# Flamingo block on one core: small loads on Sync's queue, an early activation table, score scale and gate folded into earlier operands, flag work ahead of unit 2's maxima

## The chip, the cores and the metric

The kernel runs on one core of a Trainium2 chip. The metric is device time in microseconds (us), start to end of one execution; a median of several runs is given. Lower is better. The profile is one more execution of the same program, recorded by the hardware profiler.

## The reference, cut to what matters

The input `x` is 2 x 1024 tokens of width 256. Four residual steps follow each other; the change touches the first and the two gates of the others:

```python
x = x + jnp.tanh(g_xattn[0]) * xattn0(_layernorm(x), ctx, ctx, W, b)   # one head, q = k = v projection
x = x + jnp.tanh(g_ffn[0])   * ffn0(_layernorm(x), Wg, Wu, Wd)          # 8 experts of 1024, all of them summed
x = x + jnp.tanh(g_xattn[1]) * xattn1(_layernorm(x), ctx, mask, ...)    # 8 heads, masked keys
x = x + jnp.tanh(g_ffn[1])   * moe1(_layernorm(x), wg, W, b)            # top-1 routing
# xattn0:
q, k, v = query @ W.T + b, key @ W.T + b, value @ W.T + b
weights = softmax(q @ k.T / sqrt(256)); out = weights @ v
```

The context has 154 rows for each of the two batches. `tanh(g_ffn)` is multiplied by a flag for each batch that says whether its mask leaves any key.

## The kernel before, in words

The 2048 tokens are 16 tiles of 128 rows; four tiles make a unit, so there are four units (u = 0 to 3). The kernel has five instruction streams written out by hand, one for each engine, tied by semaphores; each stream runs strictly in its written order. There are three stages: the first attention (0 to about 54 us), the dense experts of the first feed-forward (54 to about 999 us, 64 groups of matmuls in split precision), and the second attention with the routed experts (to the end).

First attention. Keys and values are the same projection k0 of the context, so the scores are computed as normalised x times A0 = W^T k0, plus a row r0 = b k0. The order of work at the start:

- Sync's queue issues the load of W0 (L495), of x unit by unit (L497) and of the first two quarters of expert weights (L506 to L508).
- ScalarE's stream issues eight loads (L893 to L900: context, bias, two gate rows, gamma, beta, gate weights, mask), then copies the transposed weight (W0T, L904) and half of the transposed context (ctxT, L906) out of PSUM, adds the bias into half of k0T (L909), takes tanh of the gates (L911, after all six loads counted by `small_in`), normalises unit 0 (L916, with rstd and shift that GpSimd makes, L601 and L603), copies half of A0 (L966), xnT (L923), V0 (L970), and for each unit the exponentials (L929) and the transposed probabilities (L936).
- TensorE runs some matmuls without use to keep busy (L1270), transposes W0 (L1278) and the context (L1283), makes k0T (L1290), r0 (L1323) and A0 (L1327), transposes unit 0 (L1296) and the values (L1314), then for each unit scores (L1340 adds r0, L1345), transposes of the probabilities (L1353) and the attention itself (L1360). The scores of unit u wait for the additions of unit u-2 (`a_res`).
- VectorE copies the other half of ctxT (L1921), takes the variances of each unit (L1879, L1883, L1886), makes the other half of k0T (L1925), splits r0 into three bfloat16 rows (L1929 to L1936), copies half of A0 (L1938), takes the maxima of the scores (L1947) and scales them (L1952), forms the coefficient tanh(g)/den (L1959, L1961) and adds the attention to x (L1968). The flag work (L1989 to L1995, here behind `a_maxes(2)` and `ln2_variances(0)`) reduces the mask and multiplies the gates. L1978, L464 and L490 prepare the first operands of the experts.
- GpSimd copies the bias rows (L590), takes powers for the normalisations (L595, L601), converts the mask (`mask_rows`, L753), and splits the first experts' weights into high and low parts (L619 to L632, and w_lo in L642, L644, L648).

Of the kernel before, what the change touches and what calls it, by code (L numbers as in the profile page):

```python
# [16 lines left out]
F32 = mybir.dt.float32  # L17
# [72 lines left out]
def flamingo_kernel(nc, x, ctx, mask, g_xattn, g_ffn, W0, b0, Wg, Wu, Wd, gamma, beta, Wq, Wkv, Wout, wgate, We, be, out):  # L90
# [55 lines left out]
    NORMED0, A0_OUT, V0_OUT, NORMED20 = 5, 6, 8, 9  # L146
# [31 lines left out]
    with ExitStack() as stack:  # L178
# [63 lines left out]
        nmA, nmsA, denA, rdenA, coefA = (sa.take(n, [P, NT], F32) for n in ("nmA", "nmsA", "denA", "rdenA", "coefA"))  # L242
# [3 lines left out]
        sr = Arena(nc, sa.at - 4 * CT * D, sa.at)  # L246
        bcol_rows = sr.take("bcol_rows", [P, KB, R_ROWS], F32)
# [246 lines left out]
        def _(sp):  # L494
# [3 lines left out]

            def load_weights(q):
# [60 lines left out]
        def _(pool):  # L560
# [29 lines left out]
            nc.gpsimd.tensor_copy(bcol_rows[:, :, 0:R_ROWS:R_MID], bcol[:].unsqueeze(2).to_broadcast([P, KB, 3])).then_inc(bias_ready, 1)  # L590
# [301 lines left out]
        def _(act):  # L892
            act.dma_start(ctx_s[:], ctx_v).then_inc(ctx_in, 16)  # L893
            act.dma_start(bcol[:], b0.rearrange("(k p) -> p k", p=P), allow_slow_non_contiguous=True).then_inc(b0_in, 16)
            act.dma_start(graw[:, 0:2], g_xattn.rearrange("(a g) -> a g", a=1).partition_broadcast(P)).then_inc(small_in, 16)
            act.dma_start(graw[:, 2:4], g_ffn.rearrange("(a g) -> a g", a=1).partition_broadcast(P)).then_inc(small_in, 16)
            act.dma_start(gammac[:], gamma.rearrange("(k p) -> p k", p=P), allow_slow_non_contiguous=True).then_inc(small_in, 16)
            act.dma_start(betac[:], beta.rearrange("(k p) -> p k", p=P), allow_slow_non_contiguous=True).then_inc(small_in, 16)
            act.dma_start(wgr[:], wgate.rearrange("(k p) e -> p k e", p=P)).then_inc(small_in, 16)
            act.dma_start(mask8[:], mask.rearrange("(a b) k -> a (b k)", a=1).partition_broadcast(P)).then_inc(small_in, 16)  # L900
# [9 lines left out]
            act.wait_ge(small_in, 96)  # L910
            nc.scalar.activation(tg[:], graw[:], ACT.Tanh).then_inc(prep_act, 1)  # L911

# [12 lines left out]
            def a_exps(u):  # L925
                act.wait_ge(a_nmax, u + 1)
                for j in range(CT):
                    n = u * CT + j
                    ins = nc.scalar.activation(PA[:, u % 2 * CT + j, :], bank[UNIT_PS[u % 2][j // 2]][:, j % 2 * 256:j % 2 * 256 + KEYS], ACT.Exp,  # L929
                                               bias=nmsA[:, n:n + 1], scale=D ** -0.5, accum_out=denA[:, n:n + 1])  # L930
# [35 lines left out]
            nc.scalar.copy(A0[:, 0, :], bank[1][:, 0:AK]).then_inc(prep_act, 1)  # L966
            a_xnT_out(0)
            for i in range(2):
# [1556 lines left out]
```

## Time and profile before

| | us |
|---|---|
| median of 3 runs | 1227.21 |
| lowest and highest | 1225.78, 1228.43 |
| profiled execution, span from the first to the last instruction | 1225.2 |
| TensorE busy in it | 1199.5 |
| VectorE busy | 1051.4 |
| GpSimd busy | 886.6 |
| ScalarE busy | 739.6 |

The span leaves out what lies ahead of the first and behind the last instruction. Busy time is summed over the span; which engine limits a stage is read from the stage, by who waits for whom. PE is TensorE's matmul, PEld its weight load, DVE VectorE, ACT ScalarE, POOL GpSimd, SP Sync; a q behind a name is that engine's sequencer or its queue of DMA issues.

### The profile page before, as it was taken

What the parts mean: (1) busy time and instruction counts of PE and PEld (TensorE: products, weight loads), DVE (VectorE), ACT (ScalarE), POOL (GpSimd) and SP (SyncE); (2) the same over time, 40 slices, a digit from 0 to 9 for tenths busy, and PEclk for the clock granted to TensorE, in tenths of its full rate; (3) what the DMA queues carried; (4) which work ended last, traced back from release to release, by engine and by line L of the source; (5) the groups of instructions that cost most, each with busy time, mean ns of one, the idle gap of its engine ahead of it and who ended that gap; (6) DMA issues with size and microseconds to landing.
All of it is one profiled execution on the core that took longest, in us unless ns stands there. A gap on an engine that the chain in (4) does not pass through costs nothing.

```text
span 1225.2 us, 18428 instructions
## 1 busy us (share of the span) xinstructions
PE 1199.5 (98%) x6143; PEld 987.8 (81%) x6143; DVE 1051.4 (86%) x1754; ACT 739.6 (60%) x1531; POOL 886.6 (72%) x848
## 2 busy tenths in 40 slices
PE   8999999999999999999999999999999998999998
PEld 6778888888888888888888888888888887777776
DVE  6887899999999999999999999999999874767556
ACT  4775566666666666666666666666666545545544
POOL 4575688888888888878888888888888626444435
PEclk9999999999999999999999999999999999999999
DMA  4020301000000000000000000011000330000131
GB/s 142 26 95 25 98 13 39 27 26 26 27 26 27 26 27 26 27 26 27 27 26 27 26 27 26 27 38 40 27 26 1 120 121 1 19 26 11 36 96 70
DMA packets 42365, 48.27 MB, mean 39 GB/s; under 512 B 4239, under 2 KB 40143, under 8 KB 42015
## 3 DMA queue, kind: packets, MB, share of 16 engines
q1 hardware_dynamic: 38992, 43.33, 10.7%
q0 software_dynamic: 1440, 3.41, 0.7%
q8 instruction: 49, 0.80, 0.3%
q10 hardware_dynamic: 1839, 0.37, 0.2%
q14 instruction: 45, 0.37, 0.1%
HBM read 37.36 MB, written 10.29 MB: 39 GB/s over the span
## 4 chain that ended last, share of the span: by engine, by line
PE 89%; DVE 5%; ACT 3%; issue 1%; ACTq 1%; POOL 0%; POOLq 0%; DVEq 0%
PE bank L1400 25%; PE bank L1402 25%; PE bank L1401 25%; ACT PC L1124 3%; PE bank L1643 2%; PE bank L1652 1%; PE bank L1822 1%; DVE nmC L2204 1%; PE bank L1805 1%; PE bank L1345 1%; PE bank L1755 1%; DVE stats L1879 1%; PE bank L1577 1%; PE bank L1627 1%; PE bank L1578 1%
## 5 line engine op out<-in xcount | busy, mean ns | idle before, releaser
L1400 PE MATMUL bank<-xop_hi,w_hi 128*128 128x512 f32 x896 | 349.2, 390 | 1.9 <-DVE half_g L2028 0.9
L1402 PE MATMUL bank<-xop_hi,w_lo 128*128 128x512 f32 x896 | 348.6, 389 | 0.0
L1401 PE MATMUL bank<-xop_lo,w_hi 128*128 128x512 f32 x896 | 348.6, 389 | 0.0
L2063 DVE TENSOR_TENSOR hid_lo<-hid,hid_hi 128x512 fp32r<-128x512 f32 x228 | 232.5, 1044 | 6.0 <-ACT hid_hi L1042 6.0
L1400 PEld LDWEIGHTS bank<-xop_hi,w_hi 128*128 128x128 f32 x896 | 168.2, 188 | 37.9 <-DVE half_g L2028 1.3
L1402 PEld LDWEIGHTS bank<-xop_hi,w_lo 128*128 128x128 f32 x896 | 168.2, 188 | 35.0
L1401 PEld LDWEIGHTS bank<-xop_lo,w_hi 128*128 128x128 f32 x896 | 168.2, 188 | 34.7
L1042 ACT CAST hid_hi<-hid 128x512 fp32r<-128x512 f32 x228 | 140.8, 622 | 63.6 <-PE bank L1402 38.3
L1026 ACT ACTIVATE s<-bank 128x512 f32<-128x512 f32 x128 | 78.2, 611 | 95.2 <-PE bank L1402 95.2
L1400 PE MATMUL bank<-hid_hi,wd_hi 128*128 128x512 f32 x344 | 134.2, 390 | 0.7 <-DVE hid_lo L2063 0.6
L1401 PE MATMUL bank<-hid_lo,wd_hi 128*128 128x512 f32 x344 | 133.9, 389 | 0.0
L1402 PE MATMUL bank<-hid_hi,wd_lo 128*128 128x512 f32 x344 | 133.9, 389 | 0.0
L1002 ACT COPY bank<-bank 128x512 f32<-128x512 f32 x128 | 73.2, 573 | 67.9 <-PE bank L1402 67.9
L2087 DVE TENSOR_TENSOR acc<-bank,acc 128x512 f32<-128x512 f32 x136 | 93.0, 684 | 20.4 <-PE bank L1402 20.3
L1032 ACT ACTIVATE half_g<-half_g 128x512 f32<-128x512 f32 x128 | 81.1, 634 | 46.8 <-DVE half_g L2036 25.5
L2055 DVE TENSOR_TENSOR hid<-half_u,half_g 128x512 f32<-128x512 f32 x128 | 107.2, 875 | 0.0
L702 POOL TENSOR_TENSOR t_loT<-t_rawT,t_hiT 128x512 fp32r<-128x512 f32 x56 | 84.2, 1526 | 16.4 <-ACT t_hiT L1049 16.4
L2046 DVE TENSOR_TENSOR hid<-bank,s 128x512 f32<-128x512 f32 x128 | 86.6, 676 | 1.2 <-PE bank L1402 1.2
L648 POOL TENSOR_TENSOR w_lo<-w_raw,w_hi 128x1024 fp32r<-128x1024 f32 x32 | 77.5, 2421 | 2.9 <-ACT w_hi L1063 2.9
L796 POOL TENSOR_TENSOR PC<-PC,rdenC 128x616 f32<-128x616 f32 x32 | 38.9, 1216 | 53.5 <-DVE rdenC L2212 53.4
L1400 PEld LDWEIGHTS bank<-hid_hi,wd_hi 128*128 128x128 f32 x344 | 64.6, 188 | 15.3 <-DVE hid_lo L2063 1.0
L1402 PEld LDWEIGHTS bank<-hid_hi,wd_lo 128*128 128x128 f32 x344 | 64.6, 188 | 13.5
(288 smaller groups left out, 2608.3 us busy)
## 6 DMA issues: line engine op xcount, KB each, us to landing
raw_gu<-in_L_ffn_Wg_dram SPq DMA_DIRECT2D x32, 256.0 KB, 2.7
raw_gu<-in_L_ffn_Wu_dram SPq DMA_DIRECT2D x32, 256.0 KB, 3.1
raw_d<-in_L_ffn_Wd_dram SPq DMA_DIRECT2D x32, 256.0 KB, 3.6
slots<-empty_row SPq DMA_DIRECT2D x1, 2080.0 KB, 11.2
xr<-slots SPq DMA_DIRECT2D x8, 260.0 KB, 4.5
x_res<-in_x_dram SPq DMA_DIRECT2D x4, 512.0 KB, 8.9
x_mid<-x_res SPq DMA_DIRECT2D x1, 2048.0 KB, 7.4
x_res<-x_mid SPq DMA_DIRECT2D x4, 512.0 KB, 5.4
```

Of the source, the lines that this page charges most:

```text
L648: nc.gpsimd.tensor_tensor(out=lo[:, :, W_S1:W_S4 + 1], in0=s[:, :, W_S1:W_S4 + 1], in1=hi[:, :, W_S1:W_S4 + 1].bitcast(F32), op=ALU.subtra ...
L702: nc.gpsimd.tensor_tensor(out=t_lo[i][:], in0=t_raw[i][:], in1=t_hi[i][:].bitcast(F32), op=ALU.subtract).then_inc(t_ready, 1)
L1026: nc.scalar.activation(out[:], ps[:], ACT.Silu).then_inc(silu_ready[h], 1)
L1032: nc.scalar.activation(half["g"][:], half["g"][:], ACT.Silu).then_inc(silu_ready[h], 1)
L1042: nc.scalar.copy(hid_hi[n % 2][h][:], hid[h][:]).then_inc(hi_ready[h], 1)
L1400: mm(ps, w, a, start=start, stop=False, skip_group_check=True)
L1401: mm(ps, w, a_low, start=False, stop=False, skip_group_check=True)
L1402: return mm(ps, w_low, a, start=False, stop=True, skip_group_check=True)
L2046: nc.vector.tensor_tensor(out=hid[h][:], in0=ps[:], in1=s[:], op=ALU.mult).then_inc(hid_ready[h], 1)
L2055: nc.vector.tensor_tensor(out=hid[h][:], in0=half["u"][:], in1=half["g"][:], op=ALU.mult).then_inc(hid_ready[h], 1)
L2063: nc.vector.tensor_tensor(out=hid_lo[n % 2][h][:], in0=hid[h][:], in1=hid_hi[n % 2][h][:].bitcast(F32), op=ALU.subtract).then_inc(lo_ready ...
L2087: nc.vector.tensor_tensor(out=to, in0=ps, in1=to, op=ALU.add).then_inc(acc_added, 1)
```

## The change

Six loads (two gate rows, mask, gamma, beta, gate weights) are issued by Sync behind the four x loads, ahead of the expert weights, instead of by ScalarE. ScalarE's stream begins, after its two remaining loads, with an exponential of one column. The tanh of the gates moves behind the copies of unit 0's transposes and ahead of the value copies. The factor 256^-0.5 goes into A0 and into the bias rows behind r0, so that the scores come out scaled, and the scaling of the maxima (L1952) goes. The first gate goes into the values V0, so that the coefficient (L1961) goes. The flag work stands ahead of unit 2's maxima. The semaphore counts of `prep_act` are renumbered. The diff, cut to its core:

```diff
@@ -143,7 +143,7 @@
     V_BANKS = ((6, 7, 0), (1, 2, 7))
     C_VALUES = 2 + HB // 2
     PREP_DVE = 4
-    NORMED0, A0_OUT, V0_OUT, NORMED20 = 5, 6, 8, 9
+    NORMED0, A0_OUT, GATES, V0_OUT, NORMED20 = 4, 5, 6, 8, 9
     R_MID, R_LOW = 32, 64
     R_ROWS = R_LOW + 1
     PREP_PE = 10
@@ -239,11 +239,12 @@
         xnT = sa.take("xnT", [P, 2, KB, CH], F32)
         PA = sa.take("PA", [P, 2 * CT, KEYS], F32)
         PTA = sa.take("PTA", [KH, 2, 2, CH], F32)
-        nmA, nmsA, denA, rdenA, coefA = (sa.take(n, [P, NT], F32) for n in ("nmA", "nmsA", "denA", "rdenA", "coefA"))
+        nmA, denA, rdenA = (sa.take(n, [P, NT], F32) for n in ("nmA", "denA", "rdenA"))
         mask8 = sa.take("mask8", [P, AK], U8, size=1)
         maskf = sa.take("maskf", [P, AK], F32)
         xnA = sa.take("xnA", [P, NT, D], F32)
         sr = Arena(nc, sa.at - 4 * CT * D, sa.at)
+        early_table = sa.take("early_table", [P, 1], F32)
         bcol_rows = sr.take("bcol_rows", [P, KB, R_ROWS], F32)
         r0_rest = sr.take("r0_rest", [R_ROWS, AK], F32)
         sums_at = sa.at + (OPERANDS_AT - sa.at) % ROW_BYTES
@@ -496,6 +497,13 @@
             for u in range(NC):
                 sp.dma_start(x_res[:, u * CT:(u + 1) * CT, :], x_v[:, u * CT:(u + 1) * CT, :]).then_inc(x_in[u], 16)
 
+            sp.dma_start(graw[:, 0:2], g_xattn.rearrange("(a g) -> a g", a=1).partition_broadcast(P)).then_inc(small_in, 16)
+            sp.dma_start(graw[:, 2:4], g_ffn.rearrange("(a g) -> a g", a=1).partition_broadcast(P)).then_inc(small_in, 16)
+            sp.dma_start(mask8[:], mask.rearrange("(a b) k -> a (b k)", a=1).partition_broadcast(P)).then_inc(small_in, 16)
+            sp.dma_start(gammac[:], gamma.rearrange("(k p) -> p k", p=P), allow_slow_non_contiguous=True).then_inc(small_in, 16)
+            sp.dma_start(betac[:], beta.rearrange("(k p) -> p k", p=P), allow_slow_non_contiguous=True).then_inc(small_in, 16)
+            sp.dma_start(wgr[:], wgate.rearrange("(k p) e -> p k e", p=P)).then_inc(small_in, 16)
+
             def load_weights(q):
                 e, f = q // (NQ // NE0), q % (NQ // NE0)
                 if q >= 2:
@@ -587,7 +595,8 @@
             nc.gpsimd.affine_select(out=before[:], in_=before[:], compare_op=ALU.is_gt, fill=0.0, base=0,
                                     pattern=[[1, P]], channel_multiplier=-1).then_inc(consts_ready, 1)
             pool.wait_ge(b0_in, 16)
-            nc.gpsimd.tensor_copy(bcol_rows[:, :, 0:R_ROWS:R_MID], bcol[:].unsqueeze(2).to_broadcast([P, KB, 3])).then_inc(bias_ready, 1)
+            nc.gpsimd.tensor_scalar(bcol_rows[:, :, 0:R_ROWS:R_MID], bcol[:].unsqueeze(2).to_broadcast([P, KB, 3]),
+                                    D ** -0.5, None, ALU.mult).then_inc(bias_ready, 1)
 
             def power(lane, n, count, first=0):
                 pool.wait_ge(var_ready[lane], count)
@@ -892,12 +901,8 @@
         def _(act):
             act.dma_start(ctx_s[:], ctx_v).then_inc(ctx_in, 16)
             act.dma_start(bcol[:], b0.rearrange("(k p) -> p k", p=P), allow_slow_non_contiguous=True).then_inc(b0_in, 16)
-            act.dma_start(graw[:, 0:2], g_xattn.rearrange("(a g) -> a g", a=1).partition_broadcast(P)).then_inc(small_in, 16)
-            act.dma_start(graw[:, 2:4], g_ffn.rearrange("(a g) -> a g", a=1).partition_broadcast(P)).then_inc(small_in, 16)
-            act.dma_start(gammac[:], gamma.rearrange("(k p) -> p k", p=P), allow_slow_non_contiguous=True).then_inc(small_in, 16)
-            act.dma_start(betac[:], beta.rearrange("(k p) -> p k", p=P), allow_slow_non_contiguous=True).then_inc(small_in, 16)
-            act.dma_start(wgr[:], wgate.rearrange("(k p) e -> p k e", p=P)).then_inc(small_in, 16)
-            act.dma_start(mask8[:], mask.rearrange("(a b) k -> a (b k)", a=1).partition_broadcast(P)).then_inc(small_in, 16)
+            act.wait_ge(pool_steps, 1)
+            nc.scalar.activation(early_table[:], ones_r[:, 0:1], ACT.Exp)
 
 
             act.wait_ge(prep_pe, 1)
@@ -907,9 +912,6 @@
             act.wait_ge(prep_pe, 5)
             act.wait_ge(b0_in, 16)
             nc.scalar.activation(k0T[:, 1, :], bank[4][:, 0:AK], ACT.Identity, bias=bcol[:, 1:2], scale=1.0).then_inc(prep_act, 1)
-            act.wait_ge(small_in, 96)
-            nc.scalar.activation(tg[:], graw[:], ACT.Tanh).then_inc(prep_act, 1)
-
             def a_norm(u, count):
                 act.wait_ge(rstd_ready[u], count)
                 for j in range(CT):
@@ -927,7 +929,7 @@
                 for j in range(CT):
                     n = u * CT + j
                     ins = nc.scalar.activation(PA[:, u % 2 * CT + j, :], bank[UNIT_PS[u % 2][j // 2]][:, j % 2 * 256:j % 2 * 256 + KEYS], ACT.Exp,
-                                               bias=nmsA[:, n:n + 1], scale=D ** -0.5, accum_out=denA[:, n:n + 1])
+                                               bias=nmA[:, n:n + 1], accum_out=denA[:, n:n + 1])
                 ins.then_inc(a_probs, 1)
 
             def a_pT_out(u):
@@ -963,11 +965,15 @@
 
             a_norm(0, 1).then_inc(prep_act, 1)
             act.wait_ge(prep_pe, 7)
-            nc.scalar.copy(A0[:, 0, :], bank[1][:, 0:AK]).then_inc(prep_act, 1)
+            nc.scalar.mul(A0[:, 0, :], bank[1][:, 0:AK], D ** -0.5).then_inc(prep_act, 1)
             a_xnT_out(0)
+            act.wait_ge(small_in, 96)
+            nc.scalar.activation(tg[:], graw[:], ACT.Tanh).then_inc(prep_act, 1)
+            act.wait_ge(prep_act, GATES)
             for i in range(2):
                 act.wait_ge(prep_pe, 9 + i)
-                nc.scalar.copy(V0[:, 2 * i:2 * i + 2, :].rearrange("p k d -> p (k d)"), bank[V0_PS[i]][0:KH, :]).then_inc(prep_act, 1)
+                nc.scalar.mul(V0[:, 2 * i:2 * i + 2, :].rearrange("p k d -> p (k d)"), bank[V0_PS[i]][0:KH, :],
+                              tg[0:KH, 0:1]).then_inc(prep_act, 1)
             a_xnT_out(1)
             a_exps(0)
             a_pT_out(0)
@@ -1935,7 +1941,7 @@
             own()
             nc.vector.tensor_tensor(out=r0[low, :], in0=r0_rest[low, :], in1=r0[low, :], op=ALU.subtract).then_inc(prep_dve, 1)
             dve.wait_ge(prep_pe, 8)
-            nc.vector.tensor_copy(A0[:, 1, :], bank[2][:, 0:AK]).then_inc(prep_dve, 1)
+            nc.vector.tensor_scalar(A0[:, 1, :], bank[2][:, 0:AK], D ** -0.5, None, ALU.mult).then_inc(prep_dve, 1)
             ln1_normed(1)
             ln1_variances(2)
 
@@ -1946,19 +1952,12 @@
                     n = u * CT + 2 * i
                     ins = nc.vector.reduce_max(nmA[:, n:n + 2], bank[UNIT_PS[u % 2][i]][:].rearrange("p (a k) -> p a k", a=2)[:, :, 0:KEYS],
                                                AX.X, negate=True)
-                steps.did(ins)
-                own()
-                us = slice(u * CT, (u + 1) * CT)
-                nc.vector.tensor_scalar(nmsA[:, us], nmA[:, us], D ** -0.5, None, ALU.mult).then_inc(a_nmax, 1)
-
-            def a_coefs(u):
+                ins.then_inc(a_nmax, 1)
+
+            def a_rdens(u):
                 us = slice(u * CT, (u + 1) * CT)
                 dve.wait_ge(a_probs, u + 1)
-                if u == 0:
-                    dve.wait_ge(prep_act, 4)
                 steps.did(nc.vector.reciprocal(rdenA[:, us], denA[:, us]))
-                own()
-                steps.did(nc.vector.tensor_scalar(coefA[:, us], rdenA[:, us], tg[:, 0:1], None, ALU.mult))
 
             def a_add_half(u, half):
                 own()
@@ -1966,11 +1965,11 @@
                 for j in range(2 * half, 2 * half + 2):
                     x = unit(u)[j]
                     ins = nc.vector.scalar_tensor_tensor(out=x, in0=bank[UNIT_PS[u % 2][half]][:, j % 2 * D:(j % 2 + 1) * D],
-                                                         scalar=coefA[:, u * CT + j:u * CT + j + 1], in1=x, op0=ALU.mult, op1=ALU.add)
+                                                         scalar=rdenA[:, u * CT + j:u * CT + j + 1], in1=x, op0=ALU.mult, op1=ALU.add)
                 ins.then_inc(a_res, 1)
 
             def a_add(u):
-                a_coefs(u)
+                a_rdens(u)
                 for half in range(2):
                     a_add_half(u, half)
 
@@ -1983,9 +1982,8 @@
             a_maxes(1)
             ln1_variances(3)
             a_add(0)
-            a_maxes(2)
-            ln2_variances(0)
             dve.wait_ge(bias_ready, MASK_READY + 1)
+            dve.wait_ge(prep_act, GATES)
             steps.did(nc.vector.reduce_max(anyv[:], maskf[:].rearrange("p (b k) -> p b k", b=B), AX.X))
             own()
             steps.did(nc.vector.reciprocal(ranyv[:], anyv[:]))
@@ -1994,6 +1992,8 @@
             own()
             steps.did(nc.vector.tensor_scalar(tg_ffn[:], tg[:, 2:4], flag[:, 0:1], flag[:, 1:2], ALU.mult, ALU.mult))
             own()
+            a_maxes(2)
+            ln2_variances(0)
             a_add(1)
             ln2_variances(1)
             a_maxes(3)
```

## Rows read from the trace of the kernel before

**Rows 1.** The page, its chain that ended last: share of the span by engine.

```profile
PE 89%; DVE 5%; ACT 3%; issue 1%; ACTq 1%; POOL 0%; POOLq 0%; DVEq 0%
```

**Rows 2.** Busy time by stretch: length, then PE, PEld, DVE, ACT, POOL, clock, DMA.

```profile
0.00:54.00 54.00, 48.19 (x274) 38.53 (x274) 38.25 (x115) 29.99 (x78) 27.10 (x67) 0.97 0.30 95
...
66.00:999.00 933.00, 932.02 (x4116) 770.84 (x4116) 855.60 (x1133) 584.20 (x1043) 746.04 (x679) 1.00 0.11 36
```

**Rows 3.** Timeline, 5 to 18 us: start, length, engine, line; in brackets idle time.

```profile
5.33 1.01 PE L1278 MATMUL bank<-ident,W0s 128*128 128x128 f32 x4
...
7.88 1.28 ACT L904 ACT_TABLE_LOAD   x1 [7.88 <-issue]
...
9.66 0.42 ACT L906 COPY ctxT<-bank 128x308 f32<-128x308 f32 x1
...
10.13 3.72 PE L1290 MATMUL bank<-ctxT,W0T 128*128 128x308 f32 x8 [2.83 <-ACT ctxT L906]
...
11.03 0.20 POOL L603 TENSOR_TENSOR shift<-shift,rstd 128x4 f32<-128x4 f32 x1
...
13.89 0.52 ACT L909 ACTIVATE k0T<-bank,bcol 128x308 f32<-128x308 f32 x1 [3.81 <-PE bank L1290]
...
14.40 2.06 ACT L916 ACTIVATE xnA<-x_res,shift,rstd 128x256 f32<-128x256 f32 x4
...
14.51 1.22 PE L1323 MATMUL bank<-k0T,bcol_rows 128*65 128x308 f32 x4
...
15.57 2.24 PE L1327 MATMUL bank<-k0T,W0s 128*128 128x308 f32 x8
```

**Rows 4.** Busy time by stretch, as rows 2, while L1290 runs.

```profile
9.60:12.90 3.30, 2.77 (x6) 1.89 (x7) 0.23 (x1) 0.48 (x2) 1.48 (x3) 0.50 1.11 342
```

**Rows 5.** Timeline, 31 to 41 us.

```profile
31.43 0.88 DVE L1968 SCALAR_TENSOR_TENSOR x_res<-bank,coefA,x_res 128x256 f32<-128x256 f32 x2 [0.18 <-PE bank L1360]
...
34.47 1.60 DVE L1952 TENSOR_SCALAR nmsA<-nmA 128x4 f32<-128x4 f32 x1
...
37.90 0.47 DVE L1989 TENSOR_REDUCE anyv<-maskf 128x2 f32<-128x308 f32 x1
...
40.62 0.29 PE L1340 MATMUL bank<-r,ones_r 65*128 65x308 bf16 x1 [1.39 <-DVE x_res L1968]
```

**Rows 6.** Timeline of VectorE, 6 to 16 us, and the second x load, with its landing.

```profile
6.91 0.48 DVE L1921 COPY ctxT<-bank 128x308 f32<-128x308 f32 x1 [6.91 <-PE bank L1283]
...
13.13 1.39 DVE L1879 BATCH_NORM_STATS2 stats<-x_res 128x6 f32<-128x256 f32 x4
...
15.77 0.47 DVE L1929 CAST r<-bank 65x308 bf16<-65x308 f32 x1 [0.63 <-PE bank L1323]
...
L497 SPq DMA_DIRECT2D x_res<-in_x_dram x1: 502/502/502, 1.8 to 1.8; - x1
...
DMA to landing us min/median/max: 8.4/8.4/8.4
```

**Rows 7.** Timeline of issues, 1 to 6 us, wgr's landing, and ScalarE at 21.74.

```profile
1.91 0.48 ACTq L895 DMA_DIRECT2D graw<-in_g_xattn_dram  x1
...
5.65 1.41 ACTq L899 DMA_DIRECT2D wgr<-in_L_ffn_wg_dram  x1
...
4.29 2.17 SPq L506 DMA_DIRECT2D raw_gu<-in_L_ffn_Wg_dram  x1
...
DMA to landing us min/median/max: 6.9/6.9/6.9
...
21.74 1.07 ACT L923 COPY xnT<-bank 128x512 f32<-128x512 f32 x2 [0.99 <-PE bank L1296]
```

**Rows 8.** Timeline of GpSimd and VectorE where they meet, 25 to 61 us.

```profile
25.41 0.72 POOL L619 TENSOR_TENSOR w_raw<-raw_gu 128x256 f32<-128x256 f32 x1 [2.10 <-DVE xnA L1892]
...
33.68 2.37 POOL L648 TENSOR_TENSOR w_lo<-w_raw,w_hi 128x1024 fp32r<-128x1024 f32 x1
...
59.78 1.20 DVE L490 TENSOR_TENSOR xop_lo<-xop_raw,xop_hi 128x512 fp32r<-128x512 f32 x1
```

## Prediction

> **What bounds the kernel now.** I read the page's chain first, then busy time by stage, then the timeline and the clock of the first 64 us. TensorE carries 89% of the chain [rows 1]. By stage this splits: from 66 to 999 us TensorE is busy 932.0 of 933.0 us, so nothing there can be shortened by this change; from 0 to 54 us it is busy 48.2 of 54.0, and the change touches only that stretch and the first microseconds after it [rows 2]. A microsecond by which the expert stage starts earlier is therefore a microsecond off the end. The question is only by how much that start, at 53.85 us, moves.
>
> The chain of the first 20 us does not begin on TensorE. ScalarE's queue hands out eight loads one after the other and only then, at 7.88 us, loads its function table and copies the transposed weight and context; TensorE waits 2.83 us for those copies, until 10.13 us [rows 3]. Behind that idle time L1290's eight matmuls run at the lower clock, granted 0.50, that is 1.2 GHz [rows 4]. They take 3.72 us, where L1327's eight of the same form take 2.24 at full clock [rows 3]. Later the chain passes through VectorE: the scaling of unit 2's maxima (L1952) takes 1.60 us, the flag work and unit 1's additions follow, and TensorE waits 1.39 us at 40.62 [rows 5].
>
> **The head, step by step.** The change takes six loads off ScalarE's queue, leaving two that end at 1.9 us [rows 7], and adds a tiny exponential that brings the table in at 1.9 to 3.2. W0T needs TensorE's L1278, done at 5.33+1.01 = 6.34; ScalarE copies W0T from 6.38 and ctxT 0.48 later, as now, until 6.86+0.42 = 7.28 [rows 3]. VectorE's half of ctxT is there at 6.91+0.48 = 7.39 [rows 6]. So L1290 starts at 7.43, 2.70 earlier. TensorE's idle time ahead of it shrinks from 2.8 us to 0.1, so I take no fall of the clock: 2.24, end at 9.67. ScalarE's k0T follows, 9.71 to 10.23, and L1323 0.10 later, at 10.33 instead of 14.51: 4.18 earlier [rows 3]. VectorE cannot follow that far. The variances of unit 1 stand ahead of r0 there, and their tile lands at 1.79+8.4 = 10.19; a transfer on Sync's queue does not move. They take 13.13 to 15.14 now, 2.01 us, so they end at 12.20, and r0's first copy starts at 12.22 instead of 15.77: **3.55 earlier** [rows 6]. A0's second half and the transposes of the values hang on that copy. ScalarE does not limit: its normalising of unit 0 waits for GpSimd until 11.23 and takes 2.06, to 13.3; A0's first half (about 0.5, as k0T) is out at 13.9, and VectorE's half comes after five more operations of r0 [rows 3].
>
> **The loads on Sync's queue.** Their six issues run from 1.91 to 7.85, 5.9 us, the longest wgr's with 1.41 [rows 3, 7]. Behind Sync's x loads the last, wgr's, would start at 4.29+5.9-1.4 = 8.8 and, landing 6.9 later, be in at 15.7. If their first took the 2.17 of the issue that stands there now, it would be 17.0 or so [rows 7]. ScalarE's tanh comes up at 15.4, the value copies are due at 16.1, and behind them is 0.99 us of idle time [rows 7]: all loads in by 16.9 costs nothing. I take 15.7, because the six carry few bytes and what they queue behind is x. Behind them on Sync stand the first experts' weights: raw_d of the first quarter is issued at 13.1 instead of 7.18 and, with the 8.4 of the x tile [rows 6], lands at 21.5, just ahead of 21.7, when GpSimd's split will ask for it (now 25.41 [rows 8]). The tanh itself (0.2) fits ahead of the value copies; with the gate as a pointer these may grow by 0.1 each, inside the 0.99. A0's factor changes no form and costs nothing; if it cost 0.1 it would sit on VectorE's path.
>
> Seen from the other side: the Trainium skill ("DMA: Bandwidth & Descriptors", Issuing engines are not separate DMA queues) says that spreading issues over engines saves only sequencer time, usually small beside the transfer. By it the move would be worth about nothing and the sum 0.5 us; the rows show 5.9 us of issues ahead of the table load, so this trace disagrees on the size.
>
> **Between 20 and 50 us.** The removed L1952 and L1961 are about 0.2 us each when free. Where GpSimd is inside an instruction they take longer and end with it: L1952's 1.60 ends at 36.07, GpSimd's w_lo (L648) at 36.05 [rows 5, 8]. The edit also moves the flag work from behind unit 2's maxima to ahead of them, and that work has the same weakness. On the new clock: unit 0's last additions end at 32.31 now [rows 5] and at 28.8 then; L1989 (0.47) and the reciprocal take VectorE to 29.45 and the flag product. GpSimd starts its split at 21.7 (3.55 of the head and 0.15 of one L1952), and its three w_lo operations, as far behind that as now, have L644 from 29.3 to 30.0 and L648 (2.37) directly behind it [rows 8]. The product has two SBUF inputs; one such operation, L490 at 59.78, took 1.20 beside GpSimd where its like takes 0.69 [rows 8]. So I let the product wait to 30.0, the long L648 go next, and L1995 wait for that, to 32.6. Unit 2's maxima end at 33.6 (two of 0.48), where now, under the head's shift alone, scaled maxima would be out at 36.07-3.55 = 32.5: a wait in place of a wait. But the flag work (1.2 us) no longer stands between them and unit 1's additions: variances (2.0) to 35.6, reciprocal to 35.8, two additions (0.88) to 36.7, and TensorE's L1340 at 36.85 instead of 40.62: **3.77**, still after a wait of 1.1 [rows 5]. From there each step (scores, transposes, attention of unit 2, L1978) repeats on TensorE. The last L1961, at 57.94, lies where VectorE feeds the first expert products: 0.27 more with its wait, nothing if TensorE were the later one there. Sum: 3.55+0.22+0.27 = **4.0 us**. The profiled span of 1225.2 would be 1221.2; the runs' median of 1227.21 lies 2.0 above that span, and I keep the distance: **1223.2 us**.
>
> The Trainium skill ("SBUF — State Buffer", the two sides of SBUF) calls the port pair that VectorE and GpSimd share an exclusive lock, held for the whole instruction, against a two-input operation too when GpSimd reads SBUF. The rows agree for the single-source form (1.60); for a product as small as the flag's no row shows it. By the rule the sum is the 4.0; without it 5.3.
>
> **The rivals.**
> B, the flag work slips through. If the product is not held, or comes 0.2 us sooner or 0.7 later relative to GpSimd, L1995 passes ahead of L648. Unit 2's maxima are then out at 31.1, the variances at 33.2, unit 1's first additions at 34.7, and L1340 starts when TensorE is free, at 35.6: 1.25 more, 5.3 in all, 1221.9 us.
> C, the clock term is not there: it falls in the new kernel too, or had not fallen in the timed runs. In the first case L1290 takes 3.72 again, the head's shift is 2.70, and 2.70+0.22+0.27 = 3.2, 1224.0; in the second 4.0-1.5 = 2.5, 1224.7. For it: one profile shows one fall. Against: the idle time ahead of it is gone.
> D, slower: Sync's queue. If each of the six issues takes 2.17 [rows 7], the last starts at 15.1 and lands at 22.0, 5.1 after it is needed, and raw_d starts at 20.1 and lands at 28.5, 6.8 after GpSimd asks. GpSimd's power for unit 3 stands behind that split, so TensorE loses about 6.8: 2.8 slower than now, 1230.0. It turns the sign from about 20.9 us for the last small load on.
> E, a remainder near nothing: the small loads in at 19 to 20.5 (2 to 3.6 lost); a table that serves the exponential but not tanh, two more loads of 1.28, where now one serves both [rows 3]; one more fall of the clock in the last stage, priced as the one in the head, 1.5; or issues that were no price (the page's rule above), 0.5, 1226.7.
>
> **How the numbers follow.** Forecast 0.38, B 0.22, C 0.18, E 0.14, D 0.08. What a measurement can tell from no change is 0.2%, 2.45 us. Faster by more: forecast, B, most of C and a little of E, 0.76; within: a rest of C and most of E, 0.15; slower 0.09. The range: B with a fall of the clock (1.5) less in the last stage gives 1220.4; C with 1.3 to 2 lost on the small loads gives 1226. I take 1220.0 to 1226.0.
>
> **What would show it.** L1290 at 7.4 and in 2.2 us, granted clock 1.00 throughout the head; r0's copy near 12.2, behind unit 1's variances; tanh near 15.5 without a wait; L1995 either 0.3 or over 2 us long; L1340 of unit 3 near 36.9 (B: 35.7); the first expert product near 50.0 and from there to the end as long as now. A wait of ScalarE for the small loads beyond 17 us, or of GpSimd for the first weights, would prove it wrong on D's side.

## The result, and the profile after

The changed kernel takes 1220.71 us (median of 4 runs, 1220.13 to 1221.10) against 1227.08 for the kernel before. The ratio is 0.9946, 95% interval 0.9935 to 0.9958. It is 6.4 us faster by the medians and 6.6 by the ratio, whose interval is 5.2 to 8.0 us. The profiled execution has a span of 1218.6 us, 6.6 less than 1225.2. The time lies inside the stated range, on the side of rival B and beyond it (1221.9).

The line of the page that answers to [rows 1], the chain by engine:

```profile
PE 89%; DVE 5%; ACT 3%; issue 1%; DMA 0%; POOL 0%; POOLq 0%; DVEq 0%; ACTq 0%
```

Nothing has become the bound in TensorE's place; only ScalarE's queue has gone from 1% to 0. Busy time by stretch, columns as in [rows 2]:

```profile
0.00:50.00 50.00, 48.23 (x282) 38.97 (x283) 35.84 (x111) 32.54 (x83) 27.27 (x67) 1.00 0.33 103
...
62.00:995.00 933.00, 932.23 (x4118) 771.12 (x4117) 853.90 (x1133) 582.56 (x1040) 744.40 (x678) 1.00 0.11 36
```

The expert stage is as full as before, 932.2 of 933. The first 50 us hold as many busy us of TensorE as the first 54 did (48.23 and 48.19; 2.2 of them are already expert products), and the granted clock is 1.00 instead of 0.97. The head, as [rows 3] and [rows 6] showed it (timeline: start, length, engine, line; the changed kernel's line numbers are 5 to 9 higher for TensorE, ScalarE and GpSimd, and differ by at most 6 for VectorE):

```profile
1.90 1.28 ACT L905 ACT_TABLE_LOAD   x1 [1.90 <-issue]
...
6.08 0.59 ACT L909 COPY W0T<-bank 128x512 f32<-128x512 f32 x1 [2.68 <-PE bank L1284]
...
7.25 2.31 PE L1296 MATMUL bank<-ctxT,W0T 128*128 128x308 f32 x8 [0.23 <-DVE ctxT L1927]
...
10.05 1.39 DVE L1885 BATCH_NORM_STATS2 stats<-x_res 128x6 f32<-128x256 f32 x4
10.28 1.22 PE L1329 MATMUL bank<-k0T,bcol_rows 128*65 128x308 f32 x4
...
11.97 0.47 DVE L1935 CAST r<-bank 65x308 bf16<-65x308 f32 x1
12.47 0.47 DVE L1937 TENSOR_TENSOR r_rest<-bank,r 65x308 f32<-65x308 f32 x1
12.98 0.35 DVE L1939 CAST r<-r_rest 1x308 bf16<-1x308 f32 x1
13.34 0.31 DVE L1940 CAST r<-r_rest 1x308 bf16<-1x308 f32 x1
...
14.19 0.48 DVE L1944 TENSOR_SCALAR A<-bank 128x308 f32<-128x308 f32 x1
...
14.82 0.59 POOL L762 CAST maskf<-mask 128x308 f32<-128x308 uint8 x1 [1.66 <-DMA wgr<-in_L_ffn_wg_dram]
...
15.10 0.22 ACT L971 ACTIVATE tg<-graw 128x4 f32<-128x4 f32 x1
```

ScalarE now waits for TensorE and no longer the other way round; k0T's matmuls run at full clock; r0's copy follows VectorE's variances of unit 1; GpSimd's mask work begins when r0 is done. Tanh does not wait: the six loads are in by 14.8, and no second table load stands ahead of it. And where TensorE waited 1.39 us [rows 5]:

```profile
27.46 1.28 POOL L651 TENSOR_TENSOR w_lo<-raw_gu,w_hi 128x512 fp32r<-128x512 f32 x1
...
28.52 0.23 DVE L1991 TENSOR_TENSOR flag<-anyv,ranyv 128x2 f32<-128x2 f32 x1
28.69 0.73 POOL L653 TENSOR_TENSOR w_lo<-raw_gu,w_hi 128x256 fp32r<-128x256 f32 x1
28.79 0.66 DVE L1993 TENSOR_SCALAR tg_ffn<-tg,flag 128x2 f32<-128x2 f32 x1
...
29.37 2.38 POOL L657 TENSOR_TENSOR w_lo<-w_raw,w_hi 128x1024 fp32r<-128x1024 f32 x1
29.48 0.86 DVE L1953 TENSOR_REDUCE nmA<-bank 128x2 f32<-128x308 f32 x2
...
33.01 0.88 DVE L1967 SCALAR_TENSOR_TENSOR x_res<-bank,rdenA,x_res 128x256 f32<-128x256 f32 x2 [0.66 <-PE bank L1366]
...
34.47 0.30 PE L1346 MATMUL bank<-r,ones_r 65*128 65x308 bf16 x1
```

The last flag operation is held for the short L653 and passes ahead of the long L657. VectorE then waits for TensorE's attention of unit 1, and L1346 of unit 3 starts without a wait. Where the microseconds arise, step by step (starts in the two profiled executions):

| step | before | after | earlier | forecast |
|---|---|---|---|---|
| k0T's matmuls | 10.13 | 7.25 | 2.88 | 2.70 |
| r0's matmuls | 14.51 | 10.28 | 4.23 | 4.18 |
| r0's first copy | 15.77 | 11.97 | 3.80 | 3.55 |
| A0's half on VectorE | 18.39 | 14.19 | 4.20 | 3.55 |
| attention of unit 0 | 27.60 | 23.20 | 4.40 | 3.6 |
| scores of unit 3 | 40.62 | 34.47 | 6.15 | 3.77 |
| first expert product | 53.85 | 47.81 | 6.04 | 3.8 |
| transposes among the products | 62.59 | 56.93 | 5.66 | 4.0 |
| end of the span | 1225.2 | 1218.6 | 6.6 | 4.0 |

### The profile page after: what moved, and what is told of

Its sections match the earlier page's. It is cut to its first block, busy times and chain, and to the rows that moved or that the text cites. A ratio compares the mean times of both kernels' runs of the same rounds, so it can differ in the third digit from the quotient of the medians.

```text
span 1218.6 us, 18422 instructions
## 1 busy us (share of the span) xinstructions
PE 1195.7 (98%) x6143; PEld 985.0 (81%) x6143; DVE 1046.2 (86%) x1746; ACT 740.1 (61%) x1532; POOL 886.6 (73%) x848
## 4 chain that ended last, share of the span: by engine, by line
PE 89%; DVE 5%; ACT 3%; issue 1%; DMA 0%; POOL 0%; POOLq 0%; DVEq 0%; ACTq 0%
PE bank L1406 25%; PE bank L1408 25%; PE bank L1407 25%; ACT PC L1130 3%; PE bank L1658 1%; PE bank L1649 1%; PE bank L1828 1%; DVE nmC L2204 1%; PE bank L1811 1%; PE bank L1366 1%; DVE stats L1885 1%; PE bank L1351 1%; PE bank L1761 1%; PE bank L1302 1%; PE bank L1583 1%
## 5 line engine op out<-in xcount | busy, mean ns | idle before, releaser
L657 POOL TENSOR_TENSOR w_lo<-w_raw,w_hi 128x1024 fp32r<-128x1024 f32 x32 | 77.5, 2422 | 2.9 <-ACT w_hi L1069 2.9
```

The costliest lines, as they stand in the source:

```text
L657: nc.gpsimd.tensor_tensor(out=lo[:, :, W_S1:W_S4 + 1], in0=s[:, :, W_S1:W_S4 + 1], in1=hi[:, :, W_S1:W_S4 + 1].bitcast(F32), op=ALU.subtra ...
```

## The experiments

All ratios are against the kernel before, run on the same chip in the same job; a job holds several experiments, and the change itself was run in the first job only. Times in brackets are starts in the profiled execution of each kernel. My theory after the result: the head is worth about 4.2 us, and what comes on top arises where VectorE and GpSimd meet around unit 2's maxima. The rival: the head alone did everything, by moving VectorE against GpSimd. No run undoes the gate in the values alone; what the missing L1961 is worth is read from the traces only.

**head_only.** The change with scaling, coefficient and place of the flag work as before:

```diff
-            nc.scalar.mul(A0[:, 0, :], bank[1][:, 0:AK], D ** -0.5).then_inc(prep_act, 1)
+            nc.scalar.copy(A0[:, 0, :], bank[1][:, 0:AK]).then_inc(prep_act, 1)
+                nc.vector.tensor_scalar(nmsA[:, us], nmA[:, us], D ** -0.5, None, ALU.mult).then_inc(a_nmax, 1)
+                steps.did(nc.vector.tensor_scalar(coefA[:, us], rdenA[:, us], tg[:, 0:1], None, ALU.mult))
```

> Only the head of the change: six small loads on Sync's queue, the early exponential, tanh behind unit 0's transposes. The scaling of the maxima, the gate in the coefficient and the place of the flag work are as before. Theory 1 (the head gives its 4.2 us, and the rest of the gain needs the removed scaling): the first expert product starts 4.2 to 4.5 us earlier than 53.85, near 49.5, unit 2's scaling again ends with GpSimd's w_lo, and the time is 4.2 to 5.3 us under before. Theory 2 (the head alone is all of it, since it also moved VectorE against GpSimd): first product at 47.8, 6.4 us under before.

Measured: 0.9966 (0.9954 to 0.9978), 1222.93 against 1227.17 us: 4.2 less, theory 1. Its timeline shows the old stall in its new place:

```profile
29.74 2.36 POOL L656 TENSOR_TENSOR w_lo<-w_raw,w_hi 128x1024 fp32r<-128x1024 f32 x1
...
30.54 1.58 DVE L1955 TENSOR_SCALAR nmsA<-nmA 128x4 f32<-128x4 f32 x1
...
36.72 0.29 PE L1343 MATMUL bank<-r,ones_r 65*128 65x308 bf16 x1 [1.42 <-DVE x_res L1971]
```

TensorE waits 1.42 us here, as it did before (1.39). The expected 49.5 for the first product was missed in this one execution (51.62): the granted clock fell behind that wait (0.66 on average from 36 to 41 us). From unit 3's scores to the first product it takes 14.90 us, against 13.23 in the kernel before; without the 1.67 it would stand at 49.95, still 0.4 later than expected.

**rest_only.** Everything but the head:

```diff
+            act.dma_start(graw[:, 0:2], ...)        # and five more, as before
-            act.wait_ge(pool_steps, 1)
-            nc.scalar.activation(early_table[:], ones_r[:, 0:1], ACT.Exp)
```

> Everything but the head: score scale in A0, gate in the values, flag work ahead of unit 2's maxima; the six loads stay on ScalarE's queue, the tanh in its old place, no early exponential. Theory 1 (the parts add up): first product 1.5 to 1.9 us earlier, near 52.1. Theory 2 (nothing without the head): within 0.3 us of before. My forecast's 0.5 us would be 53.4.

Measured: 0.9986 (0.9977 to 0.9995), 1225.29 against 1227.17 us, first product at 51.97, 1.88 earlier: theory 1. The parts add within the noise: 4.2 and 1.9 by the medians, and 6.4 together. Its k0T's matmuls take 3.99 us behind a wait of 2.38, so the fall of the clock in the head is in this execution as in that of before. My forecast had 0.5 for this part.

**flag_back, scale_back, both_back.** The change with the flag work behind unit 2's maxima again; with the scaling of the maxima on VectorE again; with both.

```diff
 # flag_back
+            a_maxes(2)
+            ln2_variances(0)
             dve.wait_ge(bias_ready, MASK_READY + 1)
 ...
-            a_maxes(2)
-            ln2_variances(0)
 # scale_back
+                nc.vector.tensor_scalar(nmsA[:, us], nmA[:, us], D ** -0.5, None, ALU.mult).then_inc(a_nmax, 1)
```

> The change with the flag work behind unit 2's maxima and unit 0's second variances again, as before. Theory 1 (with the scaling gone VectorE has room, TensorE's attention of unit 1 is the later one): L1346 of unit 3 moves by 0.2 us at most, first product near 48.0. Theory 2 (the moved flag work is what gave the extra 1.5 us behind the head): L1346 of unit 3 at 35.6 to 36.0 instead of 34.47, the time 1.2 to 1.5 us over the change.

> The change with unscaled scores and the scaling of the maxima on VectorE again (L1952 of before), flag work where the change has it. Both theories: unit 2's scaling starts near 30.35 and ends with GpSimd's w_lo near 31.75. Theory 1 (either cover alone is enough): L1346 of unit 3 at 34.8 to 34.9, 0.3 to 0.5 us later, the first product near 48.2. Theory 2 (the scaling alone gave the 1.5): 1.4 us later.

> The change with both undone: scaling of the maxima, and the flag work behind them. The gate stays in the values. Theory 1 (the two add only where neither is taken away): scaling until 31.8, variances 33.7, flag work 35.0, addition 36.0, L1346 of unit 3 near 36.1 instead of 34.47: 1.6 us later, first product near 49.4. If the effects simply added from the two single runs of theory 1, it would be 0.5 to 0.7.

Measured, with the start of unit 3's first scores and of the first product:

| | ratio to before | median us | scores of unit 3 | first product |
|---|---|---|---|---|
| the change | 0.9946 (0.9935 to 0.9958) | 1220.71 | 34.47 | 47.81 |
| flag_back | 0.9952 (0.9937 to 0.9967) | 1221.96 | 34.47 | 47.82 |
| scale_back | 0.9947 (0.9932 to 0.9962) | 1221.12 | 34.71 | 47.95 |
| both_back | 0.9970 (0.9958 to 0.9983) | 1223.48 | 36.09 | 50.92 |

The starts in the traces bear out theory 1 in all three: either part alone takes nearly everything, and only without both does TensorE wait. The medians alone would not carry this. The first row is from another job, the intervals of the first three overlap, and in the job of the other three the median of before was 1225.96, so that both_back gains 2.5 us by the medians where its ratio says 3.7. In scale_back the scaling is still held behind GpSimd, 1.38 us, and costs 0.24 at unit 3's scores. In both_back it runs into the flag work:

```profile
29.99 1.79 DVE L1957 TENSOR_SCALAR nmsA<-nmA 128x4 f32<-128x4 f32 x1
...
33.62 0.47 DVE L1991 TENSOR_REDUCE anyv<-maskf 128x2 f32<-128x308 f32 x1
...
36.09 0.42 PE L1345 MATMUL bank<-r,ones_r 65*128 65x308 bf16 x1 [1.33 <-DVE x_res L1969]
```

The first product there is 3.1 later, not the 1.6 expected, because the clock fell behind this wait, at the work that follows it; busy time by stretch of both_back, the clock is the number behind the brackets:

```profile
36.00:39.20 3.20, 3.11 (x13) 3.04 (x14) 3.06 (x12) 1.41 (x3) 1.55 (x2) 0.50 0.21 64
```

So the sum in my forecast undervalued the pair. The wait it removes is worth 1.3 us (its length) to 1.6 (the delay of unit 3's scores) by itself, and the fall of the clock about as much again in those executions in which it comes.

**before_warm.** The price of the clock in the head, with the kernel before kept busy over its wait:

```diff
-            keep_busy(2, WARM_PS)
+            keep_busy(15, WARM_PS)
             pe.wait_ge(prep_act, 2)
```

> The kernel before with 15 instead of 2 matmuls without use ahead of k0T, so that TensorE is not idle while it waits for ScalarE's copies. Theory (the fall of the clock is a price of its own in the timed runs): L1290 takes 2.2 to 2.3 us instead of 3.72 and the time is about 1.5 us under before. Rival (the fall sat only in the profiled run, or the stretch behind hides it): no difference, within 0.4 us.

Measured: 0.9991 (0.9982 to 1.0000), 1226.35 against 1227.17 us. k0T's matmuls take 2.34 us and the first product starts at 52.43, 1.42 earlier, as the theory said for the profile; at the end of the expert stage it is still 1.47 ahead (998.07 against 999.54). Its span is only 0.5 shorter, so 1.0 was given back in the last stage, and the medians show 0.8, between theory and rival. The interval runs from 0.0 to 2.2 us, so the timed runs do not decide between the two. Mean granted clocks of its runs go from 0.996 to 1.000: the fall in the head is gone, others further on come or stay away from one execution to the next.

**table_then_loads, no_early_table.** What held ScalarE's first copies: the issues, or the table load behind them? The first issues the six loads from ScalarE again, behind the exponential; the second leaves the loads with Sync and has no exponential.

```diff
 # table_then_loads
             nc.scalar.activation(early_table[:], ones_r[:, 0:1], ACT.Exp)
+            act.dma_start(graw[:, 0:2], ...)        # and five more
 # no_early_table
-            act.wait_ge(pool_steps, 1)
-            nc.scalar.activation(early_table[:], ones_r[:, 0:1], ACT.Exp)
```

> The change with the six small loads issued by ScalarE again, behind the early exponential. Theory (what held the head was the issues as a block ahead of the first copies, the table load only a part): the copies start at about 9.2, L1290 at about 10, the clock falls again; the first product is 3.5 to 4.3 us later than in the change. Rival (the table load was what held it): the copies start at about 6.1 as in the change, no loss.

> The change without the early exponential; the six loads stay on Sync's queue. Theory 1 (the table is loaded behind the wait for the transposed weight): load 6.1 to 7.4, copies until 8.3, k0T's matmuls near 8.4 instead of 7.25, r0's copy about 0.9 to 1.1 us later, and as much at the first product. Theory 2 (the load is done ahead of the wait, as soon as the queue is free): nothing is lost.

Measured: table_then_loads 0.9962 (0.9950 to 0.9974), 1222.29 us, first product at 49.40. Both of my expectations fell. The copies start at 7.84, neither at 9.2 nor at 6.1:

```profile
1.90 1.28 ACT L899 ACT_TABLE_LOAD   x1 [1.90 <-issue]
1.97 0.41 ACTq L900 DMA_DIRECT2D graw<-in_g_xattn_dram  x1
...
6.82 0.98 ACTq L905 DMA_DIRECT2D mask<-in_mask_BxS_bk_dram  x1
...
7.84 0.58 ACT L909 COPY W0T<-bank 128x512 f32<-128x512 f32 x1 [4.44 <-PE bank L1289]
...
8.80 2.34 PE L1296 MATMUL bank<-ctxT,W0T 128*128 128x308 f32 x8 [1.27 <-ACT ctxT L911]
```

The table load runs on the engine while the queue hands out the loads, although the stream has the exponential, and with it the table load, ahead of them. The order alone takes 1.34 us off (9.18 to 7.84), and the clock does not fall behind the shorter wait of 1.27. The issues themselves cost the remaining 1.76 (7.84 to 6.08), of which 1.59 is left at the first product. Without the early exponential, in the job with the low median of before: 0.9949 (0.9933 to 0.9965), 1220.53 us, first product at 47.72: nothing is lost. Its table load stands at 1.90 as well, ahead of the wait for TensorE:

```profile
1.90 1.28 ACT L907 ACT_TABLE_LOAD   x1 [1.90 <-issue]
6.51 0.59 ACT L907 COPY W0T<-bank 128x512 f32<-128x512 f32 x1 [3.32 <-PE bank L1282]
```

Theory 2: the load is placed ahead of the wait of the instruction that needs it. With the six loads gone, the added exponential is worth nothing; with them still there, it is worth 2.6 us of the head's 4.2 at the first product: the lead over before is 4.45 us in table_then_loads (53.85 to 49.40), and 1.88 of it is rest_only's.

**mask_moved.** Why r0's copies on VectorE take 2.22 us up to A0's copy (11.97 to 14.19) instead of 2.62 (15.77 to 18.39). The kernel before, with one swap on GpSimd:

```diff
-            mask_rows()
             power(2, CT, 1)
+            mask_rows()
```

> The kernel before with GpSimd's mask conversion behind the power of unit 2 instead of ahead of it, so that it no longer runs beside VectorE's copies of r0. Theory (r0's chain is 0.4 us shorter in the change because the mask work runs at another time): from r0's first copy to A0's copy 2.2 us instead of 2.62, the two 1 x 308 casts about 0.35 instead of 0.5 each, the stretch behind them 0.4 us earlier. Rival (the chain is shorter for another reason, such as the scaled form): 2.6 us as now.

Measured: 2.19 us in that stretch, and the two casts 0.31 each:

```profile
14.01 0.47 DVE L1929 CAST r<-bank 65x308 bf16<-65x308 f32 x1 [0.37 <-PE bank L1323]
14.51 0.47 DVE L1931 TENSOR_TENSOR r_rest<-bank,r 65x308 f32<-65x308 f32 x1
15.02 0.31 DVE L1933 CAST r<-r_rest 1x308 bf16<-1x308 f32 x1
15.35 0.31 DVE L1934 CAST r<-r_rest 1x308 bf16<-1x308 f32 x1
15.69 0.47 DVE L1936 TENSOR_TENSOR r<-r_rest,r 1x308 bf16<-1x308 f32 x1
16.20 0.48 DVE L1938 COPY A<-bank 128x308 f32<-128x308 f32 x1
```

The theory holds for the stretch. The median did not move, 1.0004 (0.9995 to 1.0013): 0.4 us is below what it can tell. In this profile the clock fell at unit 3's scores instead of at k0T's matmuls, although TensorE had been idle for 2.77 us ahead of the latter.

**late_small.** The changed kernel's small loads behind the first experts' weights:

```diff
             for q in range(NQ):
                 load_weights(q)
+                if q == 1:
+                    sp.dma_start(graw[:, 0:2], ...)   # and the other five
```

> The change with the six small loads behind the first two quarters of expert weights on Sync's queue instead of ahead of them. Theory (a late small load costs one for one from the slack of 0.7 us behind the value copies on): their issues begin near 9 to 11, the last lands near 17 to 19, tanh and the value copies come 2 to 4 us later, the first product 1 to 3 us later. Rival (small packets land as quickly wherever they stand): tanh by 16.2, no loss.

Measured: 0.9959 (0.9944 to 0.9974), 1222.01 us. The last load is issued at 12.93 and lands 4.3 us later. Tanh waits 1.97 us, to 17.24, and the first product is at 49.20, 1.39 late. That lies in the theory's range of 1 to 3, but the cost is not one for one: tanh is 2.14 later than in the change (15.10), the slack was to be 0.7, and only 0.68 is there at the attention of unit 0 (23.88 against 23.20). The rest comes from the flag work, which now meets GpSimd 0.45 us further on in its work and is held twice:

```profile
28.92 0.73 POOL L654 TENSOR_TENSOR w_lo<-raw_gu,w_hi 128x256 fp32r<-128x256 f32 x1
...
29.20 0.47 DVE L1992 TENSOR_TENSOR flag<-anyv,ranyv 128x2 f32<-128x2 f32 x1
29.61 2.36 POOL L658 TENSOR_TENSOR w_lo<-w_raw,w_hi 128x1024 fp32r<-128x1024 f32 x1
29.70 2.30 DVE L1994 TENSOR_SCALAR tg_ffn<-tg,flag 128x2 f32<-128x2 f32 x1
...
35.97 0.29 PE L1347 MATMUL bank<-r,ones_r 65*128 65x308 bf16 x1 [0.66 <-DVE x_res L1968]
```

This is the scene that my forecast drew for the change itself, to the instruction: the product held, L658 next, the last flag operation held for 2.30.

**a0_by_act.** An attempt at a better version, both halves of A0 on ScalarE:

```diff
-            nc.scalar.mul(A0[:, 0, :], bank[1][:, 0:AK], D ** -0.5).then_inc(prep_act, 1)
+            nc.scalar.mul(A0[:, 0, :], bank[1][:, 0:AK], D ** -0.5)
+            act.wait_ge(prep_pe, 8)
+            nc.scalar.mul(A0[:, 1, :], bank[2][:, 0:AK], D ** -0.5).then_inc(prep_act, 1)
```

> The change with both halves of A0 copied by ScalarE, so that VectorE goes from r0's last step straight to the normalising of unit 1. Theory (the transposes of the values wait for VectorE's half of A0, and ScalarE is free from 13.7 to 14.1): the transposes of the values at 14.5 instead of 14.81, first product 0.3 us earlier, 47.5. Rival (something behind takes it up, such as GpSimd's lock): first product at 47.8. By the medians 0.3 us can hardly be told.

Measured: 0.9950 (0.9936 to 0.9963), 1221.00 us, no better than the change. The first product is at 48.04, but k0T's matmuls began 0.75 later in this execution (8.00). The transposes of W0 and of the context ahead of them took 1.09 and 1.07 us instead of 0.63 and 0.70 in the change, for a reason that is not shown. Whether the 0.3 us is there stays open.

## Why the prediction was right

Right, with the likeliest mechanism in second place: 6.4 us came where 4.0 were forecast and 5.3 were rival B's. The lower end of the range had been reckoned as B together with one fall of the clock less in the last stage, 1220.4. That is what the profiled pair shows, at other prices: B's shift with 0.8 us more from the head, and 0.9 instead of 1.5 for the fall. That the time still lies 0.7 us inside the range (1220.71 against 1220.0) is partly luck, since these differences offset each other. Point by point.

**The stage.** That only the first 54 us move, and that each microsecond there is one at the end, held: 932 of 933 us in the expert stage before and after, first product 6.04 earlier, span 6.6 shorter.

**The head.** The chain of copies, matmuls at full clock and VectorE's variances came out within 0.2 us as far as r0's matmuls (4.23 against 4.18). That agreement belongs to one pair of executions: in the eight kernels whose small loads are off ScalarE's queue k0T's matmuls start between 7.25 and 8.05. r0's first copy moves much less, 11.79 to 12.28, for the variances ahead of it set it, as forecast: in flag_back k0T is 0.47 later and the copy stands at 11.97 all the same. Two terms behind them were too small. VectorE was not held by unit 1's x tile: I had let it land at 10.19 "since a transfer on Sync's queue does not move", and it landed at 8.9, 7.1 us after its issue instead of 8.4. It takes 6.9 to 7.4 in all eight kernels without the small loads on ScalarE's queue, and 8.4 to 8.8 in the five with them (before, rest_only, before_warm, table_then_loads, mask_moved). So those loads had slowed the x tiles. The copy comes 0.25 sooner than forecast, which is within the scatter above; 0.14 of it (10.05 instead of 10.19) is the tile. And r0's chain is 0.4 shorter because GpSimd's mask work, moved with its data, no longer meets it (mask_moved). I had priced the move of the mask's load only by when GpSimd needs it, not by what GpSimd's work would then stand beside.

**The flag work.** This is the step that failed. The mechanism is real: late_small shows it. The margin that B named (0.2 us sooner and the work slips through) was used up by the two terms above: attention of unit 0 ended 0.9 sooner than I had it (26.9 against 27.8), GpSimd's w_lo only 0.6 sooner (27.46 against 28.06). So the product met L651, held for 0.07, and L1993 was held only for the short L653. Unit 3's scores came 6.15 earlier instead of 3.77, of which 1.39 is the wait of [rows 5]. The grid of three experiments says more than either case: had the flag work stayed behind the maxima, nothing would have been lost, once the scaling was gone. That the order of the flag work and the scaling are each other's spare is what my sum, which followed one line through VectorE, could not show.

**The last term** came and went. L1961's 0.27 was to be gained between 54 and 61 us; instead 0.38 was lost on TensorE (6.04 to 5.66). VectorE falls behind first: its L491 at 44.48 now meets GpSimd's cast and takes 1.30, where it took 0.82:

```profile
44.20 1.04 POOL L641 CAST w_hi<-w_raw 128x1024 fp32r<-128x1024 f32 x1
44.48 1.30 DVE L491 TENSOR_TENSOR xop_lo<-xop_raw,xop_hi 128x512 fp32r<-128x512 f32 x1
```

That leaves VectorE 5.65 ahead of before. Without L1961 the additions start 5.91 earlier (52.29 against 58.20), so the 0.27 is there. The next L491 gives it back beside GpSimd: it starts 5.91 earlier than L490 of [rows 8] and ends 5.65 earlier, and TensorE's product waits for it.

```profile
52.29 1.66 DVE L1967 SCALAR_TENSOR_TENSOR x_res<-bank,rdenA,x_res 128x256 f32<-128x256 f32 x4
...
53.50 1.28 POOL L651 TENSOR_TENSOR w_lo<-raw_gu,w_hi 128x512 fp32r<-128x512 f32 x1
...
53.87 1.46 DVE L491 TENSOR_TENSOR xop_lo<-xop_raw,xop_hi 128x512 fp32r<-128x512 f32 x1
```

**The clock.** The profiled execution of the changed kernel has no fall between its start and its end; that of before had one in the head [rows 4] and one in the last stage. The second is the whole 0.9 us between 5.7 and 6.6: the lead is 5.70 us at the last of L1511's transposes (1102.53 in before) and 6.62 from 1135 on, and between them stands this stretch of before (columns as in [rows 2]), where the changed kernel has 1.00:

```profile
1108.50:1111.80 3.30, 3.30 (x27) 2.92 (x26) 2.17 (x7) 2.99 (x11) 2.43 (x2) 0.52 0.01 2
```

So of the 6.6 us between the two profiled executions about 2.3 are the clock, 1.4 in the head by before_warm and 0.9 here. The falls are a matter of the single execution: of 24 runs of before, the six with a mean clock of 0.998 or more lie between 1225.5 and 1226.6 us, the six at 0.995 between 1227.2 and 1228.6. All four runs of the change are at 0.998 or more. Against the six like ones (median 1225.84) it gains 5.1, though in another job. That the rest of the 6.4 comes from fewer waits behind which the clock can fall fits the traces, but no run tests it. Rival C had this right in kind, and its price of 1.5 in the profile (1.42 in before_warm); the medians of before_warm (0.8, interval 0.0 to 2.2) leave its price in the timed runs open.

**Sync's queue.** Rival D did not come. The six issues took 4.8 us (4.19 to 8.96) and the last load landed 6.4 after its issue, at 14.8. A first issue of 1.29 instead of 2.17 and shorter ones behind it made the difference. The forecast put a late first issue of 2.17 at 17.0 for the last load; by its own rows it is 17.4 (4.29+2.17, four more issues of together 4.0, 6.9 to landing). And a load in by 16.9 was to cost nothing: in late_small the last is in at 17.2, 0.3 past that, and 0.68 is lost at the attention of unit 0, 1.39 at the first product. So lateness has a price, and a higher one than stated. Rival E did not come either: no wait for the loads, one table for exponential and tanh, and the issues were a price (1.76 us at the copies in table_then_loads).

## What to carry to other kernels

Read what stands ahead of an engine's first instruction in its own queue: here eight loads delayed a table load that needed none of them, and the table load ahead of them gave about 2.6 of the head's 4.2 us at the first product, part of it through the clock. Before pricing a small operation on VectorE, look at which GpSimd instruction it will stand beside after the shift, not before: an operation of 0.17 or 0.29 us took 1.4 to 2.3 us beside a long one, and less than half a microsecond of alignment decides (the flag product starts 0.17 ahead of GpSimd's 128 x 256 w_lo in the change and 0.28 behind its start in late_small). When two edits cover the same wait, undo them one at a time and together; singly each may look worthless.

## What the runs showed of the hardware that was not expected

- A table load runs while the same engine's queue hands out transfers: it stood at 1.90 to 3.18 us beside issues from 1.97 on, and the engine's next copy began right behind the last issue, at 7.84. The stream has the table load ahead of these issues, and they do not wait for it. It is also done ahead of the wait of the first instruction that needs it (1.90 us, 4.6 ahead of its copy at 6.51).
- Six small loads with together some 50 KB, on a second queue, delayed a 512 KB x load issued at the same moment by 1.0 to 1.9 us (8.4 to 8.8 us to landing in five kernels with them, 6.9 to 7.4 in eight without).
- The length of one wait does not decide on the fall of the clock. It fell behind waits of TensorE of 2.83 us (k0T in before), 2.38 (k0T in rest_only), 1.33 (both_back), 1.42 (head_only) and 1.37 (unit 3's scores in mask_moved); it did not behind 2.77 (k0T in mask_moved, whose matmuls took 2.34) nor behind the 1.39 of [rows 5] or the 1.27 of table_then_loads. Behind the changed kernel's shorter waits the profile shows none.
- VectorE's 1 x 308 cast takes 0.31 to 0.35 us alone and 0.47 to 0.56 beside GpSimd's mask work, and a two-input product of 128 x 2 elements was held too (0.47 instead of 0.16, late_small), which no row of before had shown.
